# Front stage of a graph-layer kernel: seven loads of the aggregate moved from the head of ScalarE's program into its first seven turns

## The reference, cut to what matters

```python
xn = _layernorm(x)
x = x + _L0_gnn_ref(xn, edge_index, ...) + _L0_mix_ref(xn[None], ...)[0]
x = x + _L0_ffn_ref(_layernorm(x)[None], ...)[0]

# _L0_gnn_ref: relu(x @ self_w.T + self_b + segment_sum(x[col], row) @ neigh_w.T + neigh_b)
# _L0_mix_ref, after the attention sums are known:
sa = _flow_attention(_layernorm(x, g1, be1), Wq, bq, ...)[0]
x = x + sa
h = _layernorm(x, g2, be2)
h = gelu(h @ W1 + b1) @ W2 + b2
return x + h
```

## Time and profile before

| | |
|---|---|
| median of 3 runs | 3397.6 us (3396.29 to 3398.46) |
| the profiled execution, its own time | 3401.0 us |
| span from first to last instruction in it | 3399.3 us |
| busy share of the span | PE 84%, VectorE 66%, POOL 67%, ScalarE 18% |
| granted TensorE clock over the span | 0.92 of full |
| front stage | from 1195.6 us to 1501.4 us + 0.7 us (last `XMe`) |
| `agg` loads | 7, each 1792 KB |

### The profile page before, as it was taken

The page is one execution under the profiler, slowest core; times in us unless marked ns, Lnnn a source line. Parts: engine busy times, 40 slices in busy tenths (PEclk is TensorE's granted clock), DMA queues, the critical chain, the costliest instruction groups (busy, mean ns, idle before and its releaser), DMA issues. The chain is left out here.

```text
span 3399.3 us, 49751 instructions
## 1 busy us (share of the span) xinstructions
PE 2864.6 (84%) x11444; PEld 1833.4 (54%) x11445; DVE 2230.7 (66%) x3576; ACT 609.6 (18%) x1075; POOL 2261.5 (67%) x2868
## 2 busy tenths in 40 slices
PE   5869999899788749978888888888886785599898
PEld 2438888645477637753333333333332673488687
DVE  9945555566566437767777777767765666566566
ACT  1013333201111113410000000000000341333232
POOL 0077777688888847757777777777775870365565
PEclk7979999999899969989999999999999557799999
DMA  2414444456567363437777777777777761676464
GB/s 100 132 54 152 152 154 153 168 174 213 192 211 247 119 226 127 136 126 215 214 218 219 214 221 217 214 218 213 216 216 157 244 216 38 201 259 239 157 197 143
DMA packets 283764, 618.95 MB, mean 182 GB/s; under 512 B 57670, under 2 KB 62799, under 8 KB 283624
## 3 DMA queue, kind: packets, MB, share of 16 engines
q0 software_dynamic: 120416, 316.67, 31.6%
q1 hardware_dynamic: 135656, 249.51, 21.8%
q10 hardware_dynamic: 27552, 51.39, 4.2%
HBM read 461.65 MB, written 161.39 MB: 183 GB/s over the span
## 5 line engine op out<-in xcount | busy, mean ns | idle before, releaser
L212 POOL DMA_INDIRECT rec_d<-rec,to x782 | 886.0, 1133 | 229.2 <-issue 225.0
L1626 PE MATMUL PA<-gathered,onehot 128*128 128x512 f32 x1668 | 855.4, 628 | 161.9 <-DMA gathered<-y_d,from 132.8
L1597 POOL DMA_INDIRECT gathered<-y_d,from x834 | 804.6, 965 | 234.6 <-issue 200.7
L1712 DVE TENSOR_TENSOR agg<-agg,PA 128x512 f32 x834 | 572.4, 686 | 259.4 <-PE PA L1626 201.2
L1626 PEld LDWEIGHTS PA<-gathered,onehot 128*128 128x128 f32 x1668 | 275.9, 190 | 678.4 <-DVE agg L1712 383.6
L2407 DVE TENSOR_TENSOR ZLm<-PTZm,ZHm 128x512 fp32r<-128x512 f32 x112 | 77.5, 692 | 143.4 <-ACT ZHm L2385 143.4
L1699 DVE TENSOR_TENSOR onehot<-PC,row_f 128x768 f32<-128x768 f32 x139 | 132.2, 951 | 55.9 <-PE PA L1626 45.2
L2340 PE MATMUL PHm<-e_hi,ZHm 128*128 x448 | 137.7, 307 | 5.0 <-DVE ZLm L2407 4.4
L2304 POOL DMA_INDIRECT ZX<-zx_d,from_m x112 | 111.3, 994 | 28.4 <-issue 19.7
L2340 PE MATMUL PHm<-e_hi,ZLm 128*128 x448 | 126.3, 282 | 0.0
L2340 PE MATMUL PHm<-e_lo,ZHm 128*128 x448 | 126.2, 282 | 0.0
(11 more groups left out here) (448 smaller groups left out, 6700.8 us busy)
## 6 DMA issues: line engine op xcount, KB each, us to landing
Qc<-q_d SPq DMA_DIRECT2D x14, 1792.0 KB, 16.8
Kc<-k_d SPq DMA_DIRECT2D x14, 1792.0 KB, 10.7
gathered<-y_d,from POOLq DMA_INDIRECT x834, 3.8
xn_d<-XN SPq DMA_DIRECT2D x49, 256.0 KB
q_d<-Q SPq DMA_DIRECT2D x49, 256.0 KB, 2.0
k_d<-K SPq DMA_DIRECT2D x49, 256.0 KB
v_d<-V SPq DMA_DIRECT2D x49, 256.0 KB, 2.0
XNc<-xn_d ACTq DMA_DIRECT2D x49, 256.0 KB, 5.9
```

Of the source, the lines that this page charges most:

```text
L212: e.indirect_dma_start(dest, bass.IndirectOffsetOnAxis(to[s][0:rows, j:j + 1], 0), rec[s][0:rows, 2 * j:2 * j + 2], None).then_inc(scat.se ...
L1597: e.indirect_dma_start(gathered[s][j][:, :], None, y_d, bass.IndirectOffsetOnAxis(from8[s][:, j:j + 1], 0))\
L1626: e.matmul(PA[j][:, :], onehot[s][:, j, :], gathered[s][j][:, :], start=True, stop=True)\
L1712: e.tensor_tensor(rows, rows, PA[j][:, :], ALU.add).then_inc(f_add.sem, 1)
```

## The change

The seven loads leave the head of ScalarE's list. They become a step of its own, `load_agg`, which is called last in each turn and issues load t in turn t, for t from 0 to 6. So that these turns are known numbers, seven more turns are written out ahead of the loop (`peel=AGG_LOADS`), and since the new step is 0 ahead, where the smallest of the others was 1, one more still.

```diff
             @block.scalar
             def _(e):
-                for i in range(AGG_LOADS):
-                    n = TILES // AGG_LOADS
-                    e.dma_start(agg[:, i * n * D:(i + 1) * n * D].rearrange("p (t d) -> p t d", d=D),
-                                self_d[i * n * P:(i + 1) * n * P, :].rearrange("(t p) d -> p t d", p=P))\
-                        .then_inc(s_agg, 16)
                 e.wait_ge(s_in4, 16 * 9)
...
-                stages(e, FRONT, (1, high_u), (1, gelu), (4, high_q), (1, high_hidden))
+                def load_agg(t, s):
+                    if isinstance(t, int) and t < AGG_LOADS:
+                        n = TILES // AGG_LOADS
+                        e.dma_start(agg[:, t * n * D:(t + 1) * n * D].rearrange("p (t d) -> p t d", d=D),
+                                    self_d[t * n * P:(t + 1) * n * P, :].rearrange("(t p) d -> p t d", p=P))\
+                            .then_inc(s_agg, 16)
+
+                stages(e, FRONT, (1, high_u), (1, gelu), (4, high_q), (1, high_hidden), (0, load_agg), peel=AGG_LOADS)
```

## The result

The changed kernel takes 3418.88 us (median of 4 runs, 3415.55 to 3421.39), the kernel before in the same series 3396.94 us (4 runs, 3392.07 to 3398.46). The ratio is 1.0068, with an interval of 1.0055 to 1.008: 0.7% slower, 21.9 us. The forecast was 3405 with a range up to 3411, so the sign was right and the size was not. The profiled execution took 3421.39 us (span 3419.6 us, clock 0.921).

The account below looks back on a forecast made before the run. It took late weights to bound the set-up and a VectorE-SP ring, waiting for the store, to bound the turns. Terms -17.1 - 1.3 + 25.9 = +7.5 us on 3397.6 gave 3405.1, stated as 3405, range 3390 to 3411.

Parts of the forecast that it names:

- Weights earlier: Front stage set-up: without agg the nine SP loads land at 1203.4 in place of 1215.04, 11.6 us gained.
- ScalarE free: Set-up: high parts start with the weights' landing, PE's row sums then end it; 10.6 us in place of 16.1, 5.5 gained.
- the first table load: First turn: the table load that held UH back now lies behind UH, 1.3 us saved.
- Table loads in the loop: Loop's body, every second turn: removing them gains 0 us, since the store ends the wait; at best 3.6 us.
- the ring: Front stage's turns: XMe, its store on SP, sum_up, next XMe; said to bound the turn at 7.88 us, 8.02 on average.
- The store behind the large load: Turns 0 to 6: each store, issued 1.0 us behind the agg load, lands 3.7 us later, 7 x 3.7 = 25.9 us lost.
- Afterwards 7.9 to 8.0 us a turn: Sign to look for: turns behind the seven with an agg load are back at 7.9 to 8.0 us.
- Rival "fair sharing": DMA engines alternate between queues, so each of seven stores loses only 0.7 us, 4.9 us in all; 3384, chance 0.18.
- a point of decision: Delay of one store, 18.4 / 7 = 2.6 us, at which the case decides.
- Rival "clock": TensorE's clock dips in longer waits; if PE gets on the path, +5 us, 3410; chance 0.12 together with late weights.
- PE's gap ahead of `PHT`: Sign to look for: PE idles about 4 us there in the seven load turns, where it was 0.27 us.
- The range: Whole kernel: 3390 to 3411 us, leaving out most of the fair sharing case and the extremes.

Follow-up runs that it names:

- e9: Kernel before, with agg loaded in 24 pairs of tiles and one tile on SP behind the store, and sum_up writing to two own buffers; 3357.21 us, ratio 0.9898.
- e11: e9 plus an empty step that takes the table loads out of ScalarE's loop; 3344.7 us, ratio 0.9857 to the kernel before.
- e2: Changed kernel with the seven agg loads on SP's queue right behind the store; 3384.39 us, ratio 0.9976 to the kernel before.
- e5: Changed kernel with the agg load two steps earlier in ScalarE's turn, behind gelu; 3413.9 us, ratio 1.0057 to the kernel before.
- e7: Changed kernel with the loads still on ScalarE's queue but issued behind the store of the turn before; 3392.17 us, ratio 0.9989 to the kernel before.
- e8: Changed kernel with sum_up writing to two own buffers, so only mixed waits for the store; 3353.22 us, ratio 0.9875 to the kernel before.
- after: The changed kernel itself, with the seven agg loads in ScalarE's turns 0 to 6; 3418.88 us, ratio 1.0068 to the kernel before.
- e1: Kernel before with only an empty step that writes out eight more ScalarE turns, agg loads still at the head; 3396.02 us, ratio 1.0012.
- e3: Changed kernel with agg loaded in 24 pairs of tiles and one tile on SP behind the store; 3380.17 us, ratio 0.9964 to the kernel before.
- e6: Changed kernel with five extra unread products on PE in each of turns 1 to 7; 3418.51 us, ratio 1.0067 to the kernel before.
- e10: Kernel before with only sum_up writing to two own buffers; 3373.53 us, ratio 0.9942.
- e4: Changed kernel with agg loaded in 24 pairs of tiles and one tile on ScalarE behind HH, turns 2 to 26; 3425.99 us, ratio 1.0099 to the kernel before.

## Why the prediction was wrong in size

- **Weights earlier** (taken as 1203.4 in place of 1215.04, 11.6 us). Nearly right: 7.3 us behind the first issue in place of 17.5, 10.2 us.
- **ScalarE free** (5.5 us). Right: 5.5 (16.1 us from the landing to the last bias row before, 10.6 now). The bound moved to PE's row sums as said. Together 15.7 in place of 17.1, and with the first table load 17.2 in place of 18.4.
- **Table loads in the loop** (0). Right for this kernel: ten later turns, 1385.54 to 1465.48, take 7.99 us each where the mean was 8.02. e9 and e11 show that this 0 holds only as long as the store is in the ring.
- **The store behind the large load** (3.7 us, seven times, 25.9). This is the step that failed: the mechanism was right (e2, e5, e7, e8) and the term was mis-sized. It measured 5.1 us seven times, 35.7. Per turn that is 1.4 us too little, of which the rows of before account for 0.6. I carried the delay over as a difference, 7.3 less the 2.8 of a load alone, and put it on a store that alone takes 2.1 to 2.4, and I took 0.2 off because no further large load follows, which nothing bears out. But the landing is tied to the large load's issue: my pair has 7.7 us from there, less the lead of 1.2 and the 2.36 that is 4.2 us, or 29 for seven. And I read one pair of the earlier trace rows where that stage has twelve: in the six with one large load ahead the small one landed on average 7.9 us behind the large load's issue (in the six with two ahead, 8.4), which adds 0.1. The other 0.8 us a turn, some 5.5 us, are in no row of before: over the seven turns `sum_up` starts on average 8.7 us behind the load's issue, not 7.9, and why stays open. The load is also issued at the start of `HH`, not at its end (both at 1262.81), which changed the lead from 1.0 to 1.2 us.
- **Afterwards 7.9 to 8.0 us a turn.** Wrong for five turns, which lost about 3.9 us. The traces show a pattern: in "after", e1, e3 and e5 there are twelve turns without a load of 1792 KB, turn 7 behind the last of them left out, in which the clock stood at half for some 2.3 us or more between the store before and the turn's own store. In each of them the last small load left 1.24 to 1.27 us ahead of the store and `sum_up` came 3.3 to 3.8 us behind the store's issue. In the others that load leads by 2.2 us or more and `sum_up` comes after 2.1 to 3.1 us, but for turn 0, whose load leads by 1.2 us at a full clock. So a late turn lets TensorE's clock fall, the next loads leave late, and they delay the next store. That is argued, not shown: e6, with a full clock, still has one long turn, with its loads in their usual place. The cause is not settled.
- **Rival "fair sharing"**, where the store would lose 0.7 us, is refuted: 5.1 us against a point of decision of 2.6. The Trainium skill (page "DMA: Bandwidth & Descriptors", section "Queues, rings and completion order") lets each engine take turns between queues at packet granularity; no run here shows a small transfer that gets its half behind a large one, and the measured 5.1 us decide here. **Rival "clock"**: the dips came in each of the seven turns, but e6 shows that the long turns don't hang on them. PE's gap ahead of `PHT` was forecast at about 4 us; in the seven turns it was 3.3 to 6.4 us, 4.1 in the middle.
- **The range** ended at 3411, at a delay of some 4.5 us. The upper bound was one row's difference, taken as if it were the largest, and nothing was kept for what the long turns do to the turns behind them. With the delay as measured, 5.1 us, the forecast's own sum gives -18.4 + 35.7 = +17.3 us; the 3.9 us of the turns behind bring it to 21.2, against 21.9 between the medians. That the two come so close is in part luck, since the set-up gave 1.2 us less than forecast and the rest of the execution moves by some us.

Left open is why the store waits so long. A view of the changed kernel shows 391 GB/s from 1255 to 1257 and 189 from 1250 to 1252, the start of the first load; whether the large load has its packets queued ahead in each engine, or whether the store's small share is shared unevenly, none of these kernels separates.

## What to carry to other kernels

Before a large transfer is spread over the turns of a pipeline, find the small transfer whose landing ends a wait in the ring, and put the large one right behind its issue, not ahead of it: the same loads cost 5.1 us a turn ahead of the store and 1.3 behind it, whatever queue issues them. Better still is to take that transfer out of the ring: with the partial sum in buffers of its own the kernel before gained 0.6% (e10) and the changed kernel some 1.9% (e8 against "after"). A cost that is nothing today (table loads in a loop) has to be priced again whenever the wait that hides it is removed. And where a small transfer lands with a large one, count its landing from the large one's issue, over all the pairs that the trace has, rather than as a delay added to its time alone.

## What was not expected of the hardware

- Behind a 1792 KB load of another queue that was issued 1.2 us earlier, a 256 KB store landed 6.9 to 8.2 us behind its issue (by the start of `sum_up`), 2.1 to 2.4 us as a rule without one. Behind 512 KB the delay is 1.9 us, behind 1792 KB 5.1.
- Turns with no large load in them (e1) ran at 9.0 to 9.3 and 8.2 to 8.4 us in turn for seven turns, then fell back to 7.87 and 8.1. The same alternation appears in e3 (8.4 and 9.1 us), where the granted clock was 0.50 at 1374 to 1376, and in e5 behind its loads (9.1 and 8.3 us), there inside the loop. In each case it ended when the clock stayed full for two turns.
- A DMA that follows an activation in ScalarE's list was issued before the activation ended: at its start in the seven turns of "after" (0.38 us before its end), 0.24 to 0.28 us behind its start in the loop's turns of e4.
